# Gated unit of a decoder layer: squared positive part moved from VectorE to ScalarE

## The chip, the cores and the metric

One core of one Trainium2 chip runs the whole program. The metric is the device time of one execution in microseconds, the median of several. A core has five engines with a queue each, which work in order: TensorE (PE, with its weight loads as PEld), VectorE (DVE), ScalarE (ACT), GpSimd (POOL) and SyncE (SP, which issues the DMAs). They are kept in step by semaphores alone.

## The reference

A decoder of two layers on x of shape (16, 128, 128): past attention, block attention and a routed expert layer (layer 0), then a gated attention unit, a one-head attention and a top-1 expert layer (layer 1), each followed by a layer norm. The change is in the gated unit:

```python
    uv = jax.nn.silu(xn @ uv_w.T)
    u = uv[..., :E]; v = uv[..., E:2 * E]; base = uv[..., 2 * E:]      # E = 256, base 128 wide
    base = base[:, :, None, :] * gamma[None, None] + beta
    base = _rope_seq(base)
    q = base[:, :, 0]; k = base[:, :, 1]
    qk = jnp.einsum('bis,bjs->bij', q, k)
    qk = qk + w_rel[idx][None]
    kernel = jnp.square(jax.nn.relu(qk / sqrt_s))                      # 128 x 128 for each of 16 sequences
    out = u * jnp.einsum('bij,bje->bie', kernel, v)
    out = out @ o_w.T
    return x * res_scale + out
```

## The kernel before

The 16 sequences go through the late stages in 8 pairs. `late_pe`, `late_act`, `late_dve` and `late_pool` write out each engine's queue by hand: for t = 1 to LATE_STEPS each calls the `step(t)` of the gated unit (Gau), of the one-head attention (One, pair 0 at t = 8) and of the top-1 experts (Top, pair 0 at t = 16). A `step(t)` runs several stages, each on the pair t - back, and the order in its tuple is the order in the queue. Step 0 of the gated unit is done inside the last group of the routed experts (`moe.group`).

In the gated unit a pair p goes this way. ScalarE scales x (L2308, waits for GpSimd's layer norm) and, behind TensorE's transposes (L2237), copies it out of PSUM (L2316). TensorE projects it to the base (L2246), u (L2250) and v (L2254); ScalarE applies Silu to each (L2324, L2328, L2332). The rope is two products and a sum: VectorE multiplies the base by the cosine table (L2348), GpSimd multiplies its swapped half by the sine table (L2415) and adds the beta table (L2418), and VectorE adds both (L2357). TensorE forms q k (L2262) into PSUM bank 3. `kernel_matrix` on VectorE adds the relative bias (L2370) into `biased` and, after a wait for that, computes max(biased, 0) * biased into `kern` (L2375). TensorE multiplies v by it (L2273, "average"), VectorE gates the result with u (L2384), TensorE applies the output weights (L2286), and VectorE adds the kept x (L2364 keeps it, L2394 adds), with the layer norm's statistics (L1706, L1715). `biased` and `kern` have two buffers, so pair p uses that of pair p - 2.

The orders in a step t, as pair numbers relative to t:

- TensorE: project t-1, transpose x of t, average t-3, output t-4, q k of t-2;
- ScalarE: scale x of t, the three Silus of t-1, copy x of t;
- VectorE: kernel matrix t-3, add output t-5, keep t-1, cosine product t-1, rope sum t-1, gate t-3;
- GpSimd: sine product and beta t-1, and at t = 3, 4, 5 a third each of the layer norm of the last four sequences (L1767 to L1778, `late_ln_norm`), then the One stage's statistics and normalisations.

At t = 8, behind the gated unit's step, ScalarE runs a small Exp (L2879), ahead of which its table is loaded; a small Silu did the same ahead of step 0 (L1972), and a small Gelu does at t = 17 (L2882).

Of the kernel before, what the change touches and what calls it, by code (L numbers as in the profile page):

```python
# [22 lines left out]
ALU = mybir.AluOpType  # L23
ACT = mybir.ActivationFunctionType
# [37 lines left out]
def pipelined(eng, stages, count=B):  # L62


    deepest = max(lag for lag, _ in stages)
    peel = deepest + 2 + deepest % 2

    def step(n, parity):
        for lag, stage in stages:
            i = n - lag  # L70
            if not isinstance(i, int) or 0 <= i < count:
                stage(i, (parity - lag) % 2)

    for n in range(min(peel, count)):
        step(n, n)
    if peel < count:
        with eng.Fori(peel // 2, count // 2) as half:
            step(half * 2, 0)
            step(half * 2 + 1, 1)
    for n in range(count, count + deepest):  # L80
        step(n, n)
# [39 lines left out]
def declare(nc, ctx):  # L121
    c = Chip()
# [205 lines left out]
    s.own("ln2_", "aggr ln")  # L328
    for n in range(3, 7):
        s.own("ln%d_" % n, "stats aggr ln")  # L330
    s.own("gau_", "keep")
    s.own("top_", "xn")
    s.own("moe_", "xn x_turned x_t logits_prod route_d route_p exp gates_turned gates_t gates_out scaled prod out_t out_turned out "
                  + " ".join("row%d" % q for q in range(SPREAD)))
# [393 lines left out]
def attention_act(c, act, ph, more=None, tail=None):  # L728
# [58 lines left out]
    def window(t):  # L787

        if cross:
            if t in (4, 8):  # L790
                high_of("q", 0, t // 4 + 1)
            if t in (5, 9):
                high_of("k", 1, t // 4 + 1)
            if t == 7:
                copy_x(3)
            return
        if t % 4 == 0 and t < 12:
            high_of("q", 0, t // 4 + 1)
        if t % 4 == 1 and t < 12:
            high_of("k", 1, t // 4 + 1)  # L800
        if t == 6:
            high(c, act, "past_", 0, c.b_rk[:, 0:1], c.rq_parts[:, 3])
        if t in (10, 14, 16):
            high_rq({10: 0, 14: 1, 16: 2}[t])
        if t in (7, 11, 15):
            copy_out({7: 0, 11: 1, 15: 2}[t])
# [13 lines left out]
    def slot(t):  # L820
# [4 lines left out]
        if cross and t == 4:  # L825
            copy_x(2)
# [24 lines left out]
        if more:  # L851
            more(t)

    return SlotsACT(begin, slot, high_of, copy_x, copy_neg, rows, copy_norm, copy_out, high_rq)


# [937 lines left out]
def turn_bank(c, g):  # L1794

    return c.banks[:, 2 if g else 6, :]
# [120 lines left out]
class MoeACT:  # L1917
# [4 lines left out]
    def copy_x(self, g):  # L1922
        c, act, s = self.c, self.act, self.s
        act.wait_ge(*s.after("moe_x_turned", g + 1))
        self.nc.scalar.copy(c.out_T[:, g * GROUP:(g + 1) * GROUP], turn_bank(c, g)).then_inc(s["moe_x_t"], 1)
# [290 lines left out]
def lag(t, start, back):  # L2216

    p = t - start - back
    return p if 0 <= p < PAIRS else None


def both(x):

    return x.unsqueeze(1).broadcast_to([P, 2, P])


class GauPE:
# [62 lines left out]
    def step(self, t):  # L2290
        for stage, back in ((self.project, 1), (self.turn_x, 0), (self.average, 3), (self.output, 4), (self.product, 2)):
            if lag(t, 0, back) is not None:
                stage(lag(t, 0, back))


class GauACT:
# [4 lines left out]
    def scale_x(self, p):  # L2301
# [4 lines left out]
        for v in range(2):  # L2306
            i = 2 * p + v
            self.nc.scalar.activation(c.x_s[:, p % 2, v, :], column(c.Y[:, i:i + 1, :]), ACT.Identity, bias=c.shift2[:, i:i + 1],  # L2308
                                      scale=c.scale2[:, i:i + 1]).then_inc(s["gau_xs"], 1)

    def copy_x(self, p):
        c, act, s = self.c, self.act, self.s
        act.wait_ge(*s.after("gau_x_turned", p + 1))
        if p >= 2:
            act.wait_ge(*s.after("gau_v_prod", p - 1))
        self.nc.scalar.copy(c.x_T[:, p % 2, :], c.banks[:, 2, 0:PAIR]).then_inc(s["gau_x_t"], 1)  # L2316
# [15 lines left out]
        self.nc.scalar.activation(c.v2[:, p % 3].rearrange("p v e -> p (v e)"), c.banks[:, 7, :], ACT.Silu).then_inc(s["gau_v"], 1)  # L2332

    def step(self, t):
        for stage, back in ((self.scale_x, 0), (self.silu, 1), (self.copy_x, 0)):
            if lag(t, 0, back) is not None:
                stage(lag(t, 0, back))


class GauDVE:  # L2340
# [26 lines left out]
    def kernel_matrix(self, p):  # L2367
        c, dve, s = self.c, self.dve, self.s
        dve.wait_ge(*s.after("gau_qk", p + 1))
        self.nc.vector.tensor_tensor(c.biased[:, p % 2], c.banks[:, 3, 0:PAIR].rearrange("p (v t) -> p v t", v=2),  # L2370
                                     both(c.rel_bias[:, :]), ALU.add).then_inc(s["gau_biased"], 1)
        dve.wait_ge(*s.after("gau_biased", p + 1))
        if p >= 2:
            dve.wait_ge(*s.after("gau_av", p - 1))
        self.nc.vector.scalar_tensor_tensor(c.kern[:, p % 2], c.biased[:, p % 2], 0.0, c.biased[:, p % 2], ALU.max, ALU.mult)\  # L2375
            .then_inc(s["gau_kernel"], 1)

    def gate(self, p):
        c, dve, s = self.c, self.dve, self.s
# [530 lines left out]
def program(nc, a, gates, out):  # L2910
    with ExitStack() as ctx:
        c = declare(nc, ctx)
        load_first = [(c.w_qk, "w_qk"), (c.b_qk, "b_qk")]
        load_turn = [(c.ident_b, "ident_b"), (c.w_v, "w_v"), (c.b_v, "b_v"), (c.ident_f, "ident_f")]
# [230 lines left out]
```

## Time and profile before

| | |
|---|---|
| median of 3 runs | 563.93 us (561.54 to 566.16) |
| the profiled execution's own time | 562.95 us |
| its span | 560.5 us, 14081 instructions |
| VectorE busy | 453.5 us (81%), 1021 instructions |
| ScalarE busy | 334.1 us (60%), 579 instructions |
| GpSimd busy | 217.6 us (39%), 333 instructions |
| chain of waits | TensorE 66%, VectorE 16%, ScalarE 5%, GpSimd 2% |

The span runs from the first to the last instruction of the profiled execution. Busy shares are means over the whole span; the gated unit takes the stretch from about 450 to 504 us. The chain of waits is followed back from the last instruction: at each step to what released it, or to the instruction before it on its engine. A time in brackets with an arrow is idle time of the engine just before the instruction and what ended it. Merged rows (x2, x8) span from the first start to the last end.

### The profile page before, as it was taken

The page shows a single profiled execution, that of the slowest core. Times are in us where ns is not written, and L with a number is a line of the kernel's source. Part 1 is how long each engine was busy: PE and PEld are TensorE (multiplying, and loading weights), DVE is VectorE, ACT ScalarE, POOL GpSimd, SP SyncE. Part 2 cuts the span into 40 slices and gives each one's busy share as a digit, 9 for nine tenths or more (in the row PEclk, how much of TensorE's full clock was granted, in tenths as well). Part 3 has the DMA queues.
Part 4 walks back from the last instruction along what each step waited for, and adds up shares of the span by engine and source line. Part 5 has one row for each costly group of instructions (what it writes and reads, how often), then busy time and mean ns, then how long its engine had stood idle before and what let it go on. Part 6 is the DMA issues. An engine that isn't in the chain of part 4 may idle for free.

```text
span 560.5 us, 14081 instructions
## 1 busy us (share of the span) xinstructions
PE 511.9 (91%) x5230; PEld 280.6 (50%) x5230; DVE 453.5 (81%) x1021; ACT 334.1 (60%) x579; POOL 217.6 (39%) x333
## 2 busy tenths in 40 slices
PE   2799898999999999999999999889999998999894
PEld 1355563233333333333333666654544467879793
DVE  4678788889889898989884789768678757988897
ACT  3267765577787778777876767561101254446881
POOL 7213312511122421340233445064253376887543
PEclk9799999799999999999999999899999998999999
DMA  4556520230002203030302143017746800001001
GB/s 129 134 134 162 152 61 2 58 100 4 21 20 59 73 5 100 2 101 3 95 11 64 42 117 106 12 49 244 264 141 216 299 19 2 2 19 39 2 20 56
DMA packets 48303, 44.04 MB, mean 79 GB/s; under 512 B 7207, under 2 KB 39207, under 8 KB 48231
## 3 DMA queue, kind: packets, MB, share of 16 engines
q1 hardware_dynamic: 46220, 42.40, 25.7%
q10 hardware_dynamic: 2016, 0.75, 0.5%
q8 instruction: 42, 0.69, 0.5%
q14 instruction: 25, 0.20, 0.1%
HBM read 25.18 MB, written 1.18 MB: 47 GB/s over the span
## 4 chain that ended last, share of the span: by engine, by line
PE 66%; DVE 16%; issue 6%; ACT 5%; DMA 3%; POOL 2%; ACTq 1%; SPq 1%; DVEq 0%; POOLq 0%
PE banks L1240 13%; PE banks L1220 8%; PE banks L1155 5%; PE banks L1865 5%; PE banks L574 5%; PE banks L474 4%; PE banks L531 3%; DVE rec_negmax L1469 2%; DVE negmax L898 2%; PE banks L557 2%; DMA past_mem<-gates 2%; PE banks L1251 2%; DVE shared L1988 2%; ACT probs L742 1%; PE banks L2273 1%
## 5 line engine op out<-in xcount | busy, mean ns | idle before, releaser
L1469 DVE TENSOR_REDUCE rec_negmax<-banks 128x2 bf16<-128x512 f32 x256 | 164.9, 687 | 22.0 <-PE banks L1155 19.9
L1362 ACT ACTIVATE probs<-banks 128x1024 f32<-128x1024 f32 x128 | 131.0, 1024 | 47.6 <-PE banks L1220 46.7
L1155 PE MATMUL banks<-shared 62*128 62x512 bf16 x256 | 96.2, 391 | 4.2 <-DVE rec_negmax L1469 3.3
L1220 PE MATMUL banks<-shared 64*128 64x256 bf16 x512 | 97.2, 277 | 0.0
L898 DVE TENSOR_REDUCE negmax<-banks 128x8 bf16<-128x1024 f32 x64 | 78.1, 1221 | 19.2 <-PE banks L531 18.6
L1240 PE MATMUL banks<-probs,past_mem 128*32 128x256 f32 x1024 | 83.0, 396 | 1.3 <-ACT o_T L1369 1.3
L742 ACT ACTIVATE probs<-banks 128x1024 f32<-128x1024 f32 x64 | 65.1, 1018 | 27.9 <-PE banks L557 27.4
L1220 PEld LDWEIGHTS banks<-shared 64*128 64x128 bf16 x512 | 30.1, 94 | 69.6 <-issue 65.0
L1865 PE MATMUL banks<-shared,w_r 128*128 128x512 f32 x128 | 59.4, 601 | 1.5 <-DVE shared L1988 1.2
L1988 DVE TENSOR_TENSOR shared<-past_mem,out_T 128x512 f32<-128x512 f32 x64 | 43.2, 694 | 12.0 <-DMA past_mem<-gates 10.9
L574 PE MATMUL banks<-probs,shared 128*32 128x128 f32 x1024 | 42.1, 283 | 0.9 <-ACT probs L742 0.9
L531 PE MATMUL banks<-shared 62*128 62x128 bf16 x512 | 26.2, 223 | 12.3 <-DMA shared<-qk_parts 5.8
L1865 PEld LDWEIGHTS banks<-shared,w_r 128*128 128x128 f32 x128 | 22.5, 190 | 28.7 <-DVE shared L1988 15.2
L1240 PEld LDWEIGHTS banks<-probs,past_mem 128*32 128x32 f32 x1024 | 20.5, 108 | 29.7 <-issue 26.5
L1580 POOL TENSOR_TENSOR rctx<-o 128x128 f32<-128x128 f32 x16 | 7.3, 453 | 68.0 <-DVE o L1491 67.7
L1155 PEld LDWEIGHTS banks<-shared 62*128 62x128 bf16 x256 | 23.6, 93 | 19.5 <-DVE rec_negmax L1469 16.7
L1734 POOL TENSOR_SCALAR ln_tmp<-mv 128x4 f32<-128x4 f32 (+1 forms) x27 | 7.9, 292 | 61.7 <-DVE mv L1715 35.6
L557 PE MATMUL banks<-shared 64*128 64x128 bf16 x512 | 25.5, 219 | 4.6 <-ACT probs L742 4.6
L574 PEld LDWEIGHTS banks<-probs,shared 128*32 128x32 f32 x1024 | 24.5, 110 | 9.5 <-ACT probs L742 1.7
L1735 POOL TENSOR_TENSOR rstd<-ln_tmp,minus_half 128x4 f32<-128x4 f32 (+1 forms) x27 | 27.0, 1000 | 2.3
L1784 POOL TENSOR_SCALAR Y<-Y,mv,rstd 128x128 f32<-128x128 f32 x32 | 27.5, 870 | 0.7
L446 POOL CAST qk_parts<-left 128x512 bf16<-128x512 f32 x14 | 8.5, 610 | 47.7 <-DVE left L427 47.7
(261 smaller groups left out, 955.2 us busy)
## 6 DMA issues: line engine op xcount, KB each, us to landing
past_mem<-gates SPq DMA_DIRECT2D x64, 256.0 KB, 4.7
shared<-qk_parts SPq DMA_DIRECT2D x84, 128.0 KB, 2.7
shared<-past_mem SPq DMA_DIRECT2D x30, 128.0 KB, 2.9
shared<-qk_parts SPq DMA_DIRECT2D x18, 64.0 KB, 2.1
shared<-rec_neg_T SPq DMA_DIRECT2D x64, 2.0 KB
Y<-in_x SPq DMA_DIRECT2D x4, 256.0 KB, 3.1
xk_T<-in_ctx_T SPq DMA_DIRECT2D x4, 256.0 KB, 3.4
w_r<-in_w_r SPq DMA_DIRECT2D x4, 256.0 KB, 3.1
```

What stands on the lines that cost most here:

```text
L531: last = nc.tensor.matmul(c.max_banks[r][:, a * P:(a + 1) * P], c.QT[64 * r:64 * r + 62, gp, j, at_:at_ + P], c.KT[64 * r:64 * r + 62, gp, ...
L557: last = nc.tensor.matmul(c.score_banks[r][:, a * P:(a + 1) * P], c.KT[64 * r:64 * r + 64, gp, j, at_:at_ + P], c.QT[64 * r:64 * r + 64, g ...
L574: last = nc.tensor.matmul(c.ctx_bank[HV * q:HV * (q + 1), half * P:(half + 1) * P], c.V_rows[:, i % 4, head_rows(8 * half + 2 * q + a)], c ...
L742: nc.scalar.activation(c.probs[:, (2 * i + half) % 4, :], c.score_pairs[0], ACT.Exp, scale=HEAD_SCALE)\
L898: nc.vector.tensor_reduce(c.negmax[:, i % 2, :].rearrange("p (r j) -> p r j", r=2)[:, :, 4 * half:4 * half + 4], c.max_pair.rearrange("p ( ...
L1155: self.nc.tensor.matmul(c.max_banks[r], c.QT[64 * r:64 * r + 62, g % 2, j, off:off + P], c.rKT[64 * r:64 * r + 62, j, :], start=True, stop ...
L1220: last = self.nc.tensor.matmul(c.score_pairs[i % 2][:, r * 512 + a * PAIR:r * 512 + (a + 1) * PAIR], c.rKT[64 * r:64 * r + 64, 2 * g + a, ...
L1240: last = self.nc.tensor.matmul(c.ctx_bank[HV * q:HV * (q + 1), past * PAIR:(past + 1) * PAIR], c.rV_rows[:, t, head_rows(8 * (g // 2) + 2 ...
L1362: nc.scalar.activation(c.probs[:, i % 4, :], c.score_pairs[i % 2], ACT.Exp, scale=HEAD_SCALE)\
L1469: self.nc.vector.tensor_reduce(out, c.max_banks[r].rearrange("p (a t) -> p a t", a=NP_PAST), AX_X, ALU.max, negate=True).then_inc(s["rec_m ...
L1865: self.nc.tensor.matmul(sum_bank(c, g), c.w_r[:, e, :], c.scaled[:, n % RING, :], start=False, stop=(e == NE - 1)).then_inc(s["moe_prod"], 1)
L1988: self.nc.vector.tensor_tensor(c.scaled[:, n % RING, :], c.gate_rows[:, n % SPREAD, :], c.out_T[:, g * GROUP:(g + 1) * GROUP], ALU.mult).t ...
```

## The change

VectorE keeps the sum with the bias. The product max(biased, 0) * biased is replaced by two ScalarE activations of 128x256, Relu from `biased` to `kern` and Square of `kern` in place. They stand in ScalarE's queue behind the scaling of x and ahead of the Silus. VectorE waits, ahead of the sum, for Relu of two pairs before (a new semaphore `gau_relu`), as ScalarE does for the average of two pairs before.

```diff
-    s.own("gau_", "keep")
+    s.own("gau_", "keep relu")
...
 class GauACT:
+    def kernel_matrix(self, p):
+        c, act, s = self.c, self.act, self.s
+        act.wait_ge(*s.after("gau_biased", p + 1))
+        if p >= 2:
+            act.wait_ge(*s.after("gau_av", p - 1))
+        kern = c.kern[:, p % 2].rearrange("p v t -> p (v t)")
+        self.nc.scalar.activation(kern, c.biased[:, p % 2].rearrange("p v t -> p (v t)"), ACT.Relu).then_inc(s["gau_relu"], 1)
+        act.wait_ge(*s.after("gau_relu", p + 1))
+        self.nc.scalar.activation(kern, kern, ACT.Square).then_inc(s["gau_kernel"], 1)
...
     def step(self, t):
-        for stage, back in ((self.scale_x, 0), (self.silu, 1), (self.copy_x, 0)):
+        for stage, back in ((self.scale_x, 0), (self.kernel_matrix, 3), (self.silu, 1), (self.copy_x, 0)):
...
 class GauDVE:
     def kernel_matrix(self, p):
         dve.wait_ge(*s.after("gau_qk", p + 1))
+        if p >= 2:
+            dve.wait_ge(*s.after("gau_relu", p - 1))
         self.nc.vector.tensor_tensor(c.biased[:, p % 2], c.banks[:, 3, 0:PAIR].rearrange("p (v t) -> p v t", v=2),
                                      both(c.rel_bias[:, :]), ALU.add).then_inc(s["gau_biased"], 1)
-        dve.wait_ge(*s.after("gau_biased", p + 1))
-        if p >= 2:
-            dve.wait_ge(*s.after("gau_av", p - 1))
-        self.nc.vector.scalar_tensor_tensor(c.kern[:, p % 2], c.biased[:, p % 2], 0.0, c.biased[:, p % 2], ALU.max, ALU.mult)\
-            .then_inc(s["gau_kernel"], 1)
```

## Rows read from the trace of the kernel before

**Rows 1.** The page: busy us, share of the span, instructions.
```profile
PE 511.9 (91%) x5230; PEld 280.6 (50%) x5230; DVE 453.5 (81%) x1021; ACT 334.1 (60%) x579; POOL 217.6 (39%) x333
```

**Rows 2.** Windows: busy of PE, PEld, DVE, ACT, POOL; PEclk, DMA share, GB/s.
```profile
485.00:490.00 5.00, 4.38 (x31) 3.91 (x30) 4.86 (x13) 1.72 (x4) 4.76 (x5) 1.00 0.02 5
```

**Rows 3.** Timeline of VectorE: start us, us, engine, line, operation, tiles [idle before].
```profile
462.28 1.64 DVE L2357 TENSOR_TENSOR shared<-shared 128x512 f32<-128x512 f32 x1
463.84 0.41 DVE L2370 TENSOR_TENSOR shared<-banks,rel_bias 128x256 f32<-128x256 f32 x1
...
473.43 0.69 DVE L2357 TENSOR_TENSOR shared<-shared 128x512 f32<-128x512 f32 x1 [2.57 <-POOL shared L2418]
474.04 0.68 DVE L2384 SCALAR_TENSOR_TENSOR shared<-banks,shared 128x512 f32<-128x512 f32 x1
474.64 0.41 DVE L2370 TENSOR_TENSOR shared<-banks,rel_bias 128x256 f32<-128x256 f32 x1
...
486.37 0.41 DVE L2370 TENSOR_TENSOR shared<-banks,rel_bias 128x256 f32<-128x256 f32 x1
486.82 0.42 DVE L2375 SCALAR_TENSOR_TENSOR shared<-shared 128x256 f32<-128x256 f32 x1
487.16 0.60 DVE L2394 SCALAR_TENSOR_TENSOR Y<-Y,rstd,banks 128x128 f32<-128x128 f32 x2
...
492.22 0.41 DVE L2370 TENSOR_TENSOR shared<-banks,rel_bias 128x256 f32<-128x256 f32 x1
...
496.95 0.41 DVE L2370 TENSOR_TENSOR shared<-banks,rel_bias 128x256 f32<-128x256 f32 x1
...
500.40 0.42 DVE L2370 TENSOR_TENSOR shared<-banks,rel_bias 128x256 f32<-128x256 f32 x1 [0.65 <-PE banks L2262]
```

**Rows 4.** Chain of waits in order of time: start us, us, what.
```profile
497.39 0.44 DVE shared L2375
497.87 1.16 PE banks L2273 x8
...
502.19 0.89 PE banks L2273 x8
```

**Rows 5.** By line: duration ns min/median/max, first and last start us, forms.
```profile
L2415 POOL TENSOR_TENSOR shared<-shared,rope_sin x8: 1272/1476/1718, 454.9 to 491.5; 128x512 f32<-128x512 f32 x8
L2418 POOL TENSOR_TENSOR shared<-shared,rope_beta x8: 1262/1268/1597, 456.7 to 492.9; 128x512 f32<-128x512 f32 x8
L2316 ACT COPY shared<-banks x8: 367/368/380, 446.8 to 487.5; 128x256 f32<-128x256 f32 x8
L1972 ACT ACT_TABLE_LOAD  x1: 1283/1283/1283, 436.6 to 436.6; - x1
```

**Rows 6.** Timeline of ScalarE.
```profile
480.27 0.88 ACT L2308 ACTIVATE shared<-Y,shift,scale 128x128 f32<-128x128 f32 x2 [3.10 <-POOL shift L1778]
481.05 0.57 ACT L2324 ACTIVATE shared<-banks 128x512 f32<-128x512 f32 x1
```

**Rows 7.** Timeline of GpSimd.
```profile
461.98 1.40 POOL L2415 TENSOR_TENSOR shared<-shared,rope_sin 128x512 f32<-128x512 f32 x1 [0.75 <-ACT shared L2324]
...
472.06 1.27 POOL L2418 TENSOR_TENSOR shared<-shared,rope_beta 128x512 f32<-128x512 f32 x1
...
477.06 1.27 POOL L2418 TENSOR_TENSOR shared<-shared,rope_beta 128x512 f32<-128x512 f32 x1
...
479.98 0.20 POOL L1778 TENSOR_TENSOR shift<-ln_tmp,scale 128x4 f32<-128x4 f32 x1
481.76 1.27 POOL L2415 TENSOR_TENSOR shared<-shared,rope_sin 128x512 f32<-128x512 f32 x1 [1.58 <-issue]
```

**Rows 8.** Timeline of TensorE.
```profile
465.39 1.91 PE L2273 MATMUL banks<-shared 128*128 128x128 f32 x8 [2.18 <-DVE shared L2375]
```

**Rows 9.** Windows, columns as in rows 2.
```profile
466.00:467.00 1.00, 1.00 (x7) 1.00 (x6) 0.96 (x2) 0.00 (x0) 0.54 (x1) 0.50 0.06 16
...
468.00:469.00 1.00, 1.00 (x4) 0.82 (x4) 0.80 (x4) 0.00 (x0) 0.00 (x0) 0.50 0.00 0
```

## The prediction

> **What bounds the kernel now.** I read the page's busy shares first: TensorE 91%, VectorE 81%, ScalarE 60% [rows 1]. These are averages over stages with different limits, so they don't price a change to one stage. The edited lines work only in the gated unit, from the first sum with the bias at 463.8 us to the eighth at 500.4. The windows there show VectorE busy 4.86 of 5.00 us, TensorE 4.38 and ScalarE 1.72 [rows 2]. The timeline of VectorE gives the step: the fifth sum starts at 486.37, the sixth at 492.22, so 5.85 us, with no idle between its instructions [rows 3]. VectorE is the bound of these steps, and ScalarE has room.
>
> The chain of waits tells what the stage hands on. It goes through VectorE up to the seventh kernel matrix, which starts at 497.39, then into TensorE's products with v at 497.87, and it is still on TensorE with the eighth at 502.19 [rows 4]. From there it is TensorE work of the next stage. So the time at which the seventh average starts is what the change moves, and nothing behind it has slack to give a delay back.
>
> **The change part by part.** Eight instructions leave VectorE (L2375, 0.42 us each). In the step shown the bias sum starts at 486.37, the removed instruction at 486.82 and the next at 487.16 [rows 3]. Without a wait, the next instruction starts about 0.34 behind the sum too, so VectorE saves 0.79 - 0.34 = 0.45 us a step, 5.85 to 5.40.
>
> ScalarE gets 16 activations of 128x256 float32 from SBUF to SBUF. No such row exists. The nearest is its copy of the same shape out of PSUM, 368 ns [rows 5]; twice the columns with Silu take 0.57 [rows 6]. These are my bounds for one, and since the shape is that of the copy I take 0.40, a little for the SBUF source. Square waits for Relu, with a step of 0.04 between as from VectorE's sum to the instruction that reads it [rows 3]. The matrix is then ready 0.41 + 0.04 + 0.40 + 0.04 + 0.40 = 1.29 us after the sum starts, against 0.45 + 0.42 = 0.87 now: 0.42 later for TensorE. With the bounds it is 1.23 to 1.63. The new wait of VectorE on Relu of two pairs ago and ScalarE's wait on the average of two pairs ago are both over by a whole step, so they cost nothing. No DMA is issued or moved.
>
> Do the activations need another table? ScalarE's load takes 1283 ns [rows 5], and one lies ahead of Silu and one ahead of Exp; no row shows whether Relu and Square work with either. I take none. The Trainium skill (ScalarE: Activation LUTs, section on table sets) says that relu, copy and identity are filler in every set and does not list square there; the trace agrees for the copies, which run here between Silus.
>
> **Where it goes wrong is the place.** ScalarE's order in a step is now: scale x of pair t, kernel matrix of pair t-3, Silu of pair t-1, copy x. Behind the new wait stand the three Silus and the copy. The first Silu feeds GpSimd's two multiplies by the rope tables (L2415, L2418), these feed VectorE's rope sum (L2357), and in VectorE's order the gate (L2384) and the next bias sum stand behind that. So there is a closed loop: bias sum, kernel matrix, Silu, GpSimd, rope, gate, next bias sum. Today Silu doesn't wait for the sum, and VectorE's own work sets the step. The loop's length:
>
> - sum to the start of Silu: 0.41 + 0.04 + 0.40 + 0.04 + 0.30 = 1.19 us. Silu doesn't read the square, and activations without a dependence start about 0.10 before the last ends (two scalings of 0.88 in all from 480.27, and Silu at 481.05 [rows 6]);
> - start of Silu to start of GpSimd: 481.05 to 481.76, 0.71 [rows 6, 7];
> - GpSimd: 1.48 + 0.08 + 1.27 = 2.83, the medians of the two multiplies [rows 5] and the step between two of its instructions;
> - GpSimd's end at 472.06 + 1.27 = 473.33 to the rope sum at 473.43: 0.10 [rows 3, 7];
> - rope to gate 0.61, gate to the next sum 0.60 [rows 3].
>
> Together 6.04 us. VectorE's 5.40 fits into this, and so does TensorE (4.38 of 5 us, hence about 5.1 a step). VectorE would idle some 0.6 us a step for L2418.
>
> The sum, from the first bias sum to the seventh. The start gains: the rope sum at 462.28 took 1.64 because GpSimd had begun its next multiply at 461.98 [rows 3, 7]; that multiply now waits for Silu, so the rope takes its 0.69 and the first bias sum starts at 462.89 instead of 463.84, 0.95 earlier. Six loops are 36.2. Once there is a detour: the last four GpSimd layer norm steps of the fourth group run behind L2418 in one step and end with the shift, from 478.33 (477.06 + 1.27) to 480.18, and then the scaling of x, which stands ahead of the kernel matrix [rows 6, 7]. I take 1.5 for them without VectorE beside them, 0.09 to the scaling and 0.78 for it: Relu starts 2.37 after L2418's end, against 0.10 + 0.61 + 0.60 + 0.41 + 0.04 = 1.76 normally, so +0.6. The seventh sum starts at 462.89 + 36.2 + 0.6 = 499.7; today it starts at 496.95 [rows 3], so +2.8. The matrix comes 0.42 later behind it: +3.2 us at the average. At the eighth matrix nothing is added: it needs 1.29 behind its sum, and TensorE reaches it 1.8 us after (500.40 to 502.19 [rows 3, 4]).
>
> The profiled execution took 562.95 us, span 560.5; the median of the runs is 563.93, 1 us above, and they spread from 561.54 to 566.16. The forecast is 562.95 + 3.2 = about **566.2 us**, by the median 567.1.
>
> The bounds. Both activations lie in the loop, so with 0.37 and 0.57 it is 5.98 and 6.38: -0.4 to +2.0 over six. With GpSimd undisturbed, at its shortest times (1.27 + 0.08 + 1.26 [rows 5]), it is 0.22 less, -1.3 over six; with both multiplies at their longest (1.72 and 1.60) 0.57 more, +3.4. The detour is 0 to 1.0.
>
> The Trainium skill (ScalarE: Activation LUTs, rules for kernel authors) says to put relu, max and mul on VectorE and not on ScalarE, which speaks against this change; the trace's prices have the same sign, 0.74 us of ScalarE for 0.42 of VectorE.
>
> **The rivals.**
>
> 1. *VectorE's relief wins* (the other side). VectorE is saturated at 5.85 a step, and ScalarE is idle two thirds of the time [rows 2]. If the loop is shorter than VectorE's remaining 5.40, each of the five saturated steps gives its 0.45: -2.3 us, **560.7**. It decides at a loop of 5.40, which is 0.6 below my sum; each term has a row, and only the activations don't. Against it also: in the step where the rope sum waited, it waited 2.57 us for GpSimd although Silu was not held [rows 3]. Chance 0.15.
>
> 2. *The loop closes, but GpSimd runs undisturbed in it.* L2415 takes from 1.27 to 1.72 [rows 5], and VectorE, now idle ahead of each rope sum, disturbs it less. At its shortest times the loop is 5.82, and the loss 3.2 - 1.3 = 1.9: **564.9**. The Trainium skill (GPSIMD Engine Reference, specifications) says that GpSimd's SBUF interfaces are shared with VectorE's instructions with two SBUF inputs, and the removed instruction is one; the trace agrees in that the rope sum of two SBUF inputs took 1.64 beside L2415. Chance 0.15.
>
> 3. *TensorE's clock falls as well.* It stood idle for 2.18 us ahead of the first average, at 465.39 [rows 8], and its granted clock then was 0.50, the 1.2 GHz level, up to 469 [rows 9]: 3.6 us, in which half the work is lost, 1.8. The new order has a gap of about 0.9 us in each step and of some 1.5 ahead of the seventh average, where TensorE is the bound right after. 3.2 + 1.8 = 5.0: **568.0**. Against it: today's steps, with TensorE idle for 0.6 of 5 us, kept the clock at 1.00 [rows 2]. Chance 0.15.
>
> 4. *Table loads.* If one of the two functions isn't in Silu's table, each of six steps needs two loads inside the loop, 2.57 us: +15 on top, **582**. Chance 0.03.
>
> The forecast, with its own range of 563.5 to 569, keeps 0.52.
>
> **How the numbers follow.** About 1% (5.6 us) is what a measurement of this kernel tells from no change. Faster by that isn't in reach of any case: the eight removals are 3.6 us in all; 0.05 for what I overlook and for the scatter of the runs. Slower by over 1% needs 569.6: the table loads (0.03), half of the clock case (0.07), and in the forecast's case slow activations or a disturbed GpSimd (0.09), together 0.19. The rest, 0.76, is within 1%. The range from 561.8 to 570 leaves out most of rival 1, the table loads and a little of the others.
>
> **What would show it.** Right: Silu (L2324) starts about 1.2 us after each bias sum; Relu's idle ahead is released by VectorE; VectorE's rope sum waits for L2418 in nearly every step; the bias sums stand 6.0 us apart; the seventh average is about 3 us later, and from it on the two traces run parallel. The removed instruction's time shows as idle on VectorE and not as a shorter step. Wrong: bias sums 5.4 us apart with VectorE still full (rival 1); L2415 and L2418 at 1.27 each (rival 2); a granted clock of 0.5 near 502 us (rival 3); ACT_TABLE_LOAD more than at its present places (rival 4). Activations of 0.6 us or more from SBUF would put the time above 569.

## The result, and the profile after

| | before | after |
|---|---|---|
| median of the runs shared by the two | 563.4 us (561.54 to 566.16, 4 runs) | 570.2 us (568.23 to 573.36, 4 runs) |
| profiled execution | 562.95 us, span 560.5 | 568.23 us, span 566.3 |
| first to seventh bias sum | 33.11 us | 39.05 us |
| seventh average starts | 497.87 | 503.48 |
| from the first Silu of the gated unit to the end of the span | 106.3 us | 111.9 us |

The ratio after to before is 1.0134, interval 1.0095 to 1.0173: slower by 1.3%. The forecast was 566.2, with a range up to 570.0 and a chance of 0.19 for slower by over 1%. It had the mechanism and had it too small: 3.2 us forecast at the seventh average, 5.6 measured. Ratios here and below go by the fast executions alone (one of the kernel with the matrix behind the Silus took 974 us and is left out of its ratio), and they are not quotients of the medians printed beside them.

The last row of the table is what I use for single profiles below and call the **stretch**. The first Silu starts anywhere from 452.6 to 460.7 us in the profiled executions of this study, for reasons that lie ahead of the edited stage, so a whole span is a poor measure of an edit, and its end less that start a better one. It is still one execution each: three of the same kernel after gave 111.4, 111.9 and 113.2, and that of before holds a stretch at the lower clock [rows 9] that after's first doesn't.

The page's busy times of after, as in [rows 1]: VectorE has lost 8 instructions and 8.3 us, ScalarE has gained 16 and 4.9 us.

```profile
PE 511.2 (90%) x5230; PEld 278.9 (49%) x5230; DVE 445.2 (79%) x1013; ACT 339.0 (60%) x595; POOL 218.7 (39%) x333
```

One of the windows inside the stage, columns as in [rows 2] (length, busy of PE, PEld, DVE, ACT, POOL, granted clock, DMA share, GB/s). VectorE was busy for 4.86 of 5.00 us there and is now busy for 2.44; nobody else is full. When the bound engine loses half its work time and the steps get longer, the steps are set by a chain that goes round through several engines.

```profile
485.00:490.00 5.00, 4.54 (x30) 3.94 (x28) 2.44 (x6) 2.02 (x6) 4.33 (x4) 1.00 0.00 0
```

The chain itself, once round, in the timelines of after (start, duration, engine, line, operation, tiles, idle before). ScalarE: Relu waits for VectorE's sum, and the Silu of base (L2334) starts 476.92 - 475.70 = 1.22 us after that sum.

```profile
476.15 0.42 ACT L2317 ACTIVATE shared<-shared 128x256 f32<-128x256 f32 x1 [2.95 <-DVE shared L2382]
476.60 0.42 ACT L2319 ACTIVATE shared<-shared 128x256 f32<-128x256 f32 x1
476.92 0.58 ACT L2334 ACTIVATE shared<-banks 128x512 f32<-128x512 f32 x1
```

GpSimd: its multiply by rope_sin (L2422) starts 0.71 after that Silu, and here takes 2.03 us.

```profile
471.33 1.73 POOL L2422 TENSOR_TENSOR shared<-shared,rope_sin 128x512 f32<-128x512 f32 x1 [1.55 <-issue]
473.13 1.27 POOL L2425 TENSOR_TENSOR shared<-shared,rope_beta 128x512 f32<-128x512 f32 x1
...
477.63 2.03 POOL L2422 TENSOR_TENSOR shared<-shared,rope_sin 128x512 f32<-128x512 f32 x1 [0.94 <-POOL scale L1773]
479.74 1.26 POOL L2425 TENSOR_TENSOR shared<-shared,rope_beta 128x512 f32<-128x512 f32 x1
```

VectorE: the rope sum (L2367) idles 2.56 us for GpSimd, and behind it stand the gate (L2391) and the next bias sum (L2382). Read the cosine product (L2358) as well: in five of the six rounds between the first and the seventh sum it starts within 0.22 us of L2422. The idle time of the rope sum is far more than the 0.6 us a step that I had forecast; why is told further below.

```profile
471.23 0.69 DVE L2358 TENSOR_TENSOR shared<-shared,rope_cos 128x512 f32<-128x512 f32 x1 [0.89 <-ACT shared L2334]
474.49 0.69 DVE L2367 TENSOR_TENSOR shared<-shared 128x512 f32<-128x512 f32 x1 [2.57 <-POOL shared L2425]
475.10 0.69 DVE L2391 SCALAR_TENSOR_TENSOR shared<-banks,shared 128x512 f32<-128x512 f32 x1
475.70 0.42 DVE L2382 TENSOR_TENSOR shared<-banks,rel_bias 128x256 f32<-128x256 f32 x1
...
477.35 0.58 DVE L2374 SCALAR_TENSOR_TENSOR Y<-Y,mv,res_scale 128x128 f32<-128x128 f32 x2
477.85 0.68 DVE L2358 TENSOR_TENSOR shared<-shared,rope_cos 128x512 f32<-128x512 f32 x1
481.09 0.69 DVE L2367 TENSOR_TENSOR shared<-shared 128x512 f32<-128x512 f32 x1 [2.56 <-issue]
...
482.30 0.41 DVE L2382 TENSOR_TENSOR shared<-banks,rel_bias 128x256 f32<-128x256 f32 x1
...
502.12 0.41 DVE L2382 TENSOR_TENSOR shared<-banks,rel_bias 128x256 f32<-128x256 f32 x1
```

The bias sums start at 463.07, 469.41, 475.70, 482.30, 489.20, 495.81, 502.12 and 506.02. TensorE, which answers to [rows 4]: it idles 1.94 us ahead of the seventh average, waiting for Square.

```profile
503.48 1.16 PE L2273 MATMUL banks<-shared 128*128 128x128 f32 x8 [1.94 <-ACT shared L2319]
```

### The profile page after: what moved, and what is told of

Same layout as the page of the kernel before. It is cut to its first block and busy times, and to the rows that moved or that the text cites. A ratio compares the mean times of both kernels' runs of the same rounds, so it can differ in the third digit from the quotient of the medians.

```text
span 566.3 us, 14095 instructions
## 1 busy us (share of the span) xinstructions
PE 511.2 (90%) x5230; PEld 278.9 (49%) x5230; DVE 445.2 (79%) x1013; ACT 339.0 (60%) x595; POOL 218.7 (39%) x333
```

## The experiments

All kernels but two were timed in five rounds against the kernel before; after itself had three, and its third look is one run. "Sums" is the time from the first bias sum to the seventh in the profiled execution. In the profiles of before, of before with keep first and of the matrix behind the Silus, TensorE's granted clock fell to 0.50 for some 3 us behind the first average; in the others it didn't. What that is worth in their stretches is worked out below.

| kernel | ratio to before (interval) | stretch, us | sums, us |
|---|---|---|---|
| before | 1 | 106.3 | 33.1 |
| after | 1.0134 (1.0095 to 1.0173) | 111.9 | 39.1 |
| after, once more | 1.0105 (1.0061 to 1.0150) | 113.2 | 38.8 |
| after, third look | one run | 111.4 | 38.5 |
| matrix behind the Silus | 1.0143 (1.0097 to 1.0189) | 112.4 | 38.4 |
| before with the wait alone | 1.0075 (1.0048 to 1.0101) | 109.3 | 37.1 |
| before with the work alone | 1.0007 (0.9973 to 1.0040) | 105.7 | 32.3 |
| after, keep first | 1.0121 (1.0074 to 1.0169) | 110.9 | 38.0 |
| after, short cosine product | 1.0050 (1.0022 to 1.0077) | 107.9 | 35.9 |
| after, Silu of base first | 1.0007 (0.9982 to 1.0033) | 104.8 | 31.0 |
| after, Silu of base first, keep first | 1.0051 (1.0023 to 1.0079) | 105.6 | 31.7 |
| after, Silu of base first, gate early | 1.0011 (0.9983 to 1.0039) | 105.3 | 31.5 |
| before, keep first | 1.0012 (0.9980 to 1.0043) | 107.6 | 34.4 |

### Is it the place of the matrix in ScalarE's order?

```diff
-        for stage, back in ((self.scale_x, 0), (self.kernel_matrix, 3), (self.silu, 1), (self.copy_x, 0)):
+        for stage, back in ((self.scale_x, 0), (self.silu, 1), (self.copy_x, 0), (self.kernel_matrix, 3)):
```

> The kernel after, with the kernel matrix moved to the end of ScalarE's step, behind the three Silus and the copy; nothing else changes. Theory (the loop: the Silu stands behind the wait for the bias sum, so GpSimd's multiplies start late): the loop opens, Silu no longer waits for the sum of its own step, bias sums are 5.3 to 5.6 us apart, and the time is at or below that of the kernel before: ratio 0.995 to 1.002. Rival 1 (the two activations cost what they cost by their own time on the way to TensorE, wherever they stand): ratio 1.008 to 1.014 as in the kernel after. Rival 2 (the loss lies outside the gated unit): also 1.01.

Measured: 571.25 us, ratio 1.0143, no better than the change, so this expectation failed. The Silus no longer wait for the sum and GpSimd's multiplies are at 1.27, yet from the third on the bias sums stand 6.80 us apart. ScalarE in this kernel, one step (columns as above):

```profile
483.17 0.60 ACT L2342 ACTIVATE shared<-banks 128x512 f32<-128x512 f32 x1 [0.26 <-PE banks L2254]
483.66 0.37 ACT L2326 COPY shared<-banks 128x256 f32<-128x256 f32 x1
483.92 0.43 ACT L2317 ACTIVATE shared<-shared 128x256 f32<-128x256 f32 x1
...
488.25 0.60 ACT L2334 ACTIVATE shared<-banks 128x512 f32<-128x512 f32 x1 [2.69 <-PE banks L2246]
```

And its TensorE:

```profile
482.11 1.03 PE L2254 MATMUL banks<-w_v,shared 128*128 128x256 f32 x4
482.97 0.38 PE L2237 MATMUL banks<-ident_f,shared 128*128 128x128 f32 x2
484.85 1.16 PE L2273 MATMUL banks<-shared 128*128 128x128 f32 x8 [1.49 <-ACT shared L2319]
...
487.18 1.03 PE L2246 MATMUL banks<-shared,w_ub 128*128 128x256 f32 x4
```

Another chain has closed. The matrix stands behind the Silu of v, which waits for TensorE's product L2254; TensorE's average L2273 waits for the matrix; and the next pair's products, L2246 first, stand behind the average. One round is 6.80 us. So the place of the wait matters on both sides: behind TensorE's late products it is as bad as ahead of the Silus. The theory of the loop through Silu was neither shown nor refuted by this kernel, which needed a cleaner cut.

### How much is the wait, how much the work?

One kernel has only the wait: the kernel before, whose ScalarE waits for VectorE's finished matrix of pair t-3 where the change has its two activations.

```diff
+    def held(self, p):
+        self.act.wait_ge(*self.s.after("gau_kernel", p + 1))
...
-        for stage, back in ((self.scale_x, 0), (self.silu, 1), (self.copy_x, 0)):
+        for stage, back in ((self.scale_x, 0), (self.held, 3), (self.silu, 1), (self.copy_x, 0)):
```

> The kernel before (VectorE computes both parts of the kernel matrix), and in ScalarE's queue, where the two activations stand in the kernel after, only a wait for the kernel matrix of pair t-3. ScalarE does no work for it. Theory: the loop is closed as well, shorter by the difference of 1.22 and about 0.90 us from the bias sum to the start of Silu: about 6.0 us with GpSimd at 3.1, so some 0.3 x 6 = 2 us below the kernel after and 3 to 4 us above before: ratio 1.005 to 1.008. Rival 1 (the activations' own time): no loss, ratio 0.999 to 1.002.

Measured: 566.71 us, ratio 1.0075, stretch +3.0; the ratio is as expected. The other kernel has only the work: two activations of the same size at the same place, on a tile that needs no sum.

```diff
+    def spare(self, p):
+        act.wait_ge(*s.after("gau_square", p))
...
+        self.nc.scalar.activation(rctx, ctx, ACT.Relu).then_inc(s["gau_relu"], 1)
+        act.wait_ge(*s.after("gau_relu", p + 1))
+        self.nc.scalar.activation(rctx, rctx, ACT.Square).then_inc(s["gau_square"], 1)
...
-        for stage, back in ((self.scale_x, 0), (self.silu, 1), (self.copy_x, 0)):
+        for stage, back in ((self.scale_x, 0), (self.spare, 3), (self.silu, 1), (self.copy_x, 0)):
```

> The kernel before, with two more activations of 128x256 in ScalarE's queue where the change has them, but on a tile that is already there (Relu of ctx, Square in place), so that they wait for no sum; VectorE keeps its own square. It has ScalarE's added work without the added wait. Theory (the wait behind the sum costs, the 0.83 us of work does not): ScalarE idles over 2 us in each step, so stage from first Silu to end 106 to 107.5 us against 106.3, ratio 0.999 to 1.002. Rival (the two activations' own time costs: 8 x 0.83 us, of which what is not hidden lengthens each step): ratio 1.003 to 1.013, stage 108 to 112.

Measured: 561.24 us, ratio 1.0007, stretch 105.7. ScalarE does all the added work (its two lines, L2315 and L2317 there, have 3.3 us busy each) and it costs nothing measurable; the interval leaves room for up to 0.4%. The wait without any work costs over half of the loss.

The stretches need a correction before they are compared, because the clock fell behind the first average in before's profile and in neither of these two. First average of the kernel with the work alone:

```profile
471.02 1.16 PE L2273 MATMUL banks<-shared 128*128 128x128 f32 x8 [2.25 <-DVE shared L2383]
```

From there to the third bias sum the clock makes the difference: the first two rounds took 10.80 us in before and 10.79 in before with keep first, where it fell, and 9.30 here, where it was kept. So before's stretch would be about 104.8 without the fall, by my estimate from these rounds, and the losses are about 4.5 for the wait, 0.9 for the work and 7.1 for both. That is 1.7 more than the two alone; the two profiles of after in which the clock was kept differ by 0.5. A reason that fits, not shown by itself, is that work which is hidden beside other work isn't hidden inside a closed loop: behind the wait, Silu starts 0.90 us after the sum with the wait alone and 1.22 with both, 1.9 us over six rounds. The ratios (1.0075, 1.0007 and 1.0105 to 1.0134) point the same way, but their intervals are too wide to show it.

In the kernel with the wait alone GpSimd's two multiplies took only 1.27 us each in the step below, and still the steps were 6.0 to 6.3 us. The expectation had 3.1 us of GpSimd for that, which holds for the first two rounds alone. Its VectorE shows why; L2367 there is the keep, a pair of 128x128 instructions with two SBUF inputs:

```profile
482.34 0.41 DVE L2373 TENSOR_TENSOR shared<-banks,rel_bias 128x256 f32<-128x256 f32 x1
...
484.44 2.29 DVE L2367 SCALAR_TENSOR_TENSOR Y<-Y,mv,res_scale 128x128 f32<-128x128 f32 x2
486.66 0.68 DVE L2351 TENSOR_TENSOR shared<-shared,rope_cos 128x512 f32<-128x512 f32 x1
```

Its GpSimd in the same step:

```profile
483.97 1.27 POOL L2418 TENSOR_TENSOR shared<-shared,rope_sin 128x512 f32<-128x512 f32 x1 [1.78 <-issue]
485.32 1.27 POOL L2421 TENSOR_TENSOR shared<-shared,rope_beta 128x512 f32<-128x512 f32 x1
```

Here VectorE comes to the keep 2.10 us after the sum, 0.45 later than in after, and GpSimd to its multiply 1.63 after it, 0.30 earlier. GpSimd had begun first, and the keep took 2.29 us instead of 0.58. In after it is the other way round. One of the two engines pays.

### What does VectorE beside GpSimd cost in the loop?

The cosine product over 2 of 128 columns; the rest of its work is missing. The order and the waits are those of after.

```diff
-        self.nc.vector.tensor_tensor(c.turned[:, p % 2], ...
-                                     c.rope_cos[:, :, :].unsqueeze(2).broadcast_to([P, 2, 2, P]), ALU.mult)
+        self.nc.vector.tensor_tensor(c.turned[:, p % 2, :, :, 0:2], ...
+                                     c.rope_cos[:, :, 0:2].unsqueeze(2).broadcast_to([P, 2, 2, 2]), ALU.mult)
```

> The kernel after, with VectorE's cosine product over 2 of 128 columns (the rest of the rope is left out, so this part of the work is missing). It measures what lies beside GpSimd's multiply. Theory that the cosine product, with two SBUF inputs, lengthens the multiply from 1.27 to 1.73 us: 1.27 in the first three steps, where nothing else of VectorE lies beside it, and the loop is 0.45 shorter: 2 to 3 us below the kernel after, ratio 1.006 to 1.009. Rival (length has another source): the multiply keeps 1.7 and the time stays within 0.5 us of the kernel after, since the cosine product itself isn't in the loop.

Measured: 565.25 us, ratio 1.0050, stretch 107.9, 4.0 less than after: the direction of the theory, and somewhat more than its 2 to 3 us. Its GpSimd:

```profile
481.94 1.27 POOL L2422 TENSOR_TENSOR shared<-shared,rope_sin 128x512 f32<-128x512 f32 x1 [2.35 <-issue]
483.29 1.27 POOL L2425 TENSOR_TENSOR shared<-shared,rope_beta 128x512 f32<-128x512 f32 x1
487.82 1.43 POOL L2422 TENSOR_TENSOR shared<-shared,rope_sin 128x512 f32<-128x512 f32 x1 [1.55 <-issue]
```

Where both multiplies are at 1.27, and outside the detour, the bias sums are 5.81 to 5.83 us apart, the length that the prediction's second rival gave the loop. VectorE idled over 2 us a step in after, so the 0.5 us of work that the cut saves there can't be the gain by itself; it comes through GpSimd. Next, the order of VectorE, to take the keep out of L2422's way:

```diff
-        for stage, back in ((self.kernel_matrix, 3), (self.add_out, 5), (self.keep, 1), (self.turn, 1), (self.rope, 1), (self.gate, 3)):
+        for stage, back in ((self.kernel_matrix, 3), (self.keep, 1), (self.add_out, 5), (self.turn, 1), (self.rope, 1), (self.gate, 3)):
```

> The kernel after, with VectorE's keep moved ahead of add_out, so that it runs before GpSimd's first multiply begins. In the kernel after that multiply took 1.73 us beside the cosine product alone, and 2.03 in the two steps in which keep lay beside it too. Theory that the neighbours on VectorE lengthen GpSimd's multiply: 1.73 in all steps, 0.6 to 0.9 us less than the kernel after, ratio about 1.011 against 1.0125. Rival (the multiply's length has another source): 2.03 stays in two steps and the time too.

Measured: 569.23 us, ratio 1.0121; stretch 1.0 less than after, within the scatter of after's own three (111.4 to 113.2). The expected 1.73 in all steps came in three of the six rounds (1.77, 1.72, 1.72). No multiply takes 2.03 any more, but in the other three it is at 1.27 or 1.28 and now the cosine product pays, with 1.53 to 1.58. VectorE and then GpSimd in one step:

```profile
484.14 1.58 DVE L2358 TENSOR_TENSOR shared<-shared,rope_cos 128x512 f32<-128x512 f32 x1
```

```profile
483.90 1.27 POOL L2422 TENSOR_TENSOR shared<-shared,rope_sin 128x512 f32<-128x512 f32 x1 [0.94 <-POOL scale L1773]
485.25 1.59 POOL L2425 TENSOR_TENSOR shared<-shared,rope_beta 128x512 f32<-128x512 f32 x1
...
490.64 1.72 POOL L2422 TENSOR_TENSOR shared<-shared,rope_sin 128x512 f32<-128x512 f32 x1 [2.34 <-issue]
```

### Is one Silu all of it?

The three Silus are split: that of base goes ahead of the matrix, those of u and v stay behind it. The two activations, the wait and VectorE's shorter list are all still there.

```diff
-    def silu(self, p):
+    def silu_base(self, p):
...
+    def silu(self, p):
...
-        for stage, back in ((self.scale_x, 0), (self.kernel_matrix, 3), (self.silu, 1), (self.copy_x, 0)):
+        for stage, back in ((self.scale_x, 0), (self.silu_base, 1), (self.kernel_matrix, 3), (self.silu, 1), (self.copy_x, 0)):
```

> The kernel after, with only the Silu of the base moved ahead of the kernel matrix in ScalarE's step; the Silus of u and v and the copy stay behind it. With the matrix at the very end, the bias sums were 6.8 us apart from the fourth on and TensorE waited 1.49 us a step for Square, since the matrix stood behind the Silu of v, which waits for TensorE's products. Theory (the place in the queue costs, not the work): GpSimd starts without the bias sum, the matrix waits for one product of TensorE only, bias sums 5.3 to 5.6 us apart, first Silu to end of span 105 to 106.5 us (before 106.3, after 111.9), ratio 0.995 to 1.003. Rival (16 activations cost by their own time and place of computation): span part 109 us or more, ratio above 1.007.

Measured: 562.68 us against 562.72, ratio 1.0007 (0.9982 to 1.0033); stretch 104.8. The whole loss is gone. ScalarE of this kernel:

```profile
480.03 0.88 ACT L2308 ACTIVATE shared<-Y,shift,scale 128x128 f32<-128x128 f32 x2 [3.09 <-POOL shift L1778]
480.81 0.57 ACT L2334 ACTIVATE shared<-banks 128x512 f32<-128x512 f32 x1
481.29 0.40 ACT L2317 ACTIVATE shared<-shared 128x256 f32<-128x256 f32 x1
481.73 0.42 ACT L2319 ACTIVATE shared<-shared 128x256 f32<-128x256 f32 x1
```

Silu of base no longer stands behind the sum, so GpSimd, rope and gate don't either. This is the cleanest cut of the study: one instruction moved, 7.1 us of stretch back. The stretch is also 1.5 us below that of before, but this isn't the relief of VectorE that the first rival counted on. It is what the fall of the clock cost in before's profile; here TensorE stood idle for 2.00 us ahead of the first average and kept its clock:

```profile
466.78 1.16 PE L2273 MATMUL banks<-shared 128*128 128x128 f32 x8 [2.00 <-ACT shared L2319]
```

The first two rounds took 8.97 us here, 9.30 with the work alone and 10.80 in before; the next four took 22.03 here and 22.31 in before. So of the 2.1 us between 33.1 and 31.0 at most some 0.6 are left for the relief, and the interval of the timed executions allows for a gain of 1.0 us and a loss of 1.9.

### Is there more in the open loop?

With the loop open, VectorE's keep again took up to 2.56 us beside GpSimd. Two orders of VectorE were tried against that, and the first also on the kernel before. Keep ahead of add_out (the edit shown above), with Silu of base first:

> As the kernel with the base's Silu first, and VectorE's keep ahead of add_out. In the kernel before and in those with free steps, the pair of keeps took 1.6 to 2.7 us where GpSimd's multiply began beside it, instead of 0.6. If keep escapes the multiply, VectorE's step falls towards 5.1 us, where TensorE's own 5.1 sets it: 1 to 2 us below the kernel with the base's Silu first, ratio 0.992 to 0.999. Rival: the instruction that now stands in keep's place (the cosine product, the rope sum) is held as long instead, and nothing is gained.

Measured: 565.21 us, ratio 1.0051, slower than before. The stretch of its one profile, 105.6, doesn't show this loss, so where it lies stays open. The collisions have moved: the cosine product is held for 1.38 in one step, and the keep, in later ones, for 1.62 and 2.79 us. The same order in the kernel before:

> The kernel before, with VectorE's keep ahead of add_out and nothing else. It tells whether what the kernel before loses beside GpSimd is keep's place: if so 1 to 2 us below before, ratio 0.996 to 0.999; if another instruction is held in its stead, 0.999 to 1.002.

Measured: 564.42 us, ratio 1.0012, no difference that can be measured; one keep was held for 2.71. Then the gate ahead of the keep:

```diff
-        for stage, back in ((self.kernel_matrix, 3), (self.add_out, 5), (self.keep, 1), (self.turn, 1), (self.rope, 1), (self.gate, 3)):
+        for stage, back in ((self.kernel_matrix, 3), (self.add_out, 5), (self.gate, 3), (self.keep, 1), (self.turn, 1), (self.rope, 1)):
```

> The changed kernel with the Silu of base ahead of the matrix (as in e5_base_first), and in addition VectorE's gate of step t-3 moved ahead of the keep of step t-1. Theory (with the loop open, the sums stand 5.1 to 5.7 us apart because VectorE and GpSimd hold each other up in turn; what is moved within VectorE's order moves the hold-up elsewhere): stage from the first Silu to the end of the span 104 to 105.5 us, ratio 0.998 to 1.002, no gain over e5_base_first's 104.8. Rival (the two-input keep was what waited, and the gate, which needs only what is long done, fills its place): a stage of 103 us or less, ratio 0.994 or less, GpSimd's multiplies at 1.27 us and the keep at 0.6 us.

Measured: 561.47 us against 561.75, ratio 1.0011, stretch 105.3. The signs of the rival came, and its time did not. From the third round on the multiplies are at 1.27 or 1.28 and the keep is at 0.61 (0.74 once), and VectorE idles instead for TensorE's average, ahead of the gate:

```profile
475.25 0.69 DVE L2394 SCALAR_TENSOR_TENSOR shared<-banks,shared 128x512 f32<-128x512 f32 x1 [0.85 <-PE banks L2273]
475.86 0.61 DVE L2377 SCALAR_TENSOR_TENSOR Y<-Y,mv,res_scale 128x128 f32<-128x128 f32 x2
476.38 0.69 DVE L2361 TENSOR_TENSOR shared<-shared,rope_cos 128x512 f32<-128x512 f32 x1
477.10 0.69 DVE L2370 TENSOR_TENSOR shared<-shared 128x512 f32<-128x512 f32 x1
477.71 0.42 DVE L2385 TENSOR_TENSOR shared<-banks,rel_bias 128x256 f32<-128x256 f32 x1
```

And TensorE is full there, as far as its modelled ends tell. Columns as above:

```profile
472.00:477.00 5.00, 5.00 (x35) 4.67 (x34) 4.05 (x13) 2.67 (x6) 3.71 (x6) 1.00 0.00 2
```

Its queue goes round once in 5.04 us (the product of base starts at 471.34 and 476.38), and the bias sums stand 5.02 to 5.08 apart in four of the six rounds, with 6.05 in the step with the layer norm detour. So with VectorE's collisions gone the step is TensorE's own, about the 5.1 us that the prediction worked out for it. Six such rounds are 30.2 us by this estimate, and the kernel with the Silu of base first took 31.0 with the detour in it; no order of VectorE or ScalarE has much left to win by it. No kernel of the study is shown to be faster than the one before.

### Does TensorE's clock fall?

The change once more, as it is:

> The kernel after, unchanged, on the same chip and beside the same runs of the kernel before as the others. Its profile gave 111.9 us from the first Silu to the end of the span, against 106.3, so 5.6 us or 1.0%; the first comparison said 1.34%. If the whole loss lies in that part, the ratio is near 1.010; if something ahead of it is slower too, near 1.013 again, and the first Silu starts more than 1 us later than in the kernel before.

Measured: 568.50 us, ratio 1.0105, what the stretch alone had led me to expect. The first Silu came at 457.79 us, 3.6 later than in before, so the scatter ahead of the stage is larger than what this sign was to tell. In this profile the seventh average starts after a gap of 1.95 us and takes 2.07 us, and the granted clock is 0.50, the 1.2 GHz level, for some 3 us behind it:

```profile
506.65 2.07 PE L2273 MATMUL banks<-shared 128*128 128x128 f32 x8 [1.95 <-ACT shared L2319]
```

Windows of one us, columns as above:

```profile
507.00:508.00 1.00, 1.00 (x6) 1.00 (x6) 0.01 (x1) 0.34 (x2) 0.90 (x2) 0.50 0.00 0
...
509.00:510.00 1.00, 1.00 (x7) 1.00 (x7) 0.45 (x1) 0.00 (x0) 1.00 (x3) 0.58 0.00 0
```

The eighth sum comes 5.40 us after the seventh and not 3.90, so a fall costs 1.5 us. A third look at the same kernel:

> The changed kernel as it is, for a further look at TensorE's clock at the seventh average. If the clock falls only in some executions: the gap ahead of that average is again 1.9 to 2.0 us, and the sum of the seventh step to that of the eighth is either 3.9 us (clock kept) or 5.4 us (clock fallen). If the fall is the rule and the first profile the exception: 5.4 us again.

```profile
505.17 1.16 PE L2273 MATMUL banks<-shared 128*128 128x128 f32 x8 [1.95 <-ACT shared L2319]
```

The same gap, the clock kept, 3.89 us to the eighth sum. So behind the seventh average it fell in one of three profiled executions.

## Why the prediction was wrong

**What held.** The place in ScalarE's queue decided. The closed loop that was named is the one in the trace, Silu following the sum by 1.22 us (1.19 forecast) and the rope waiting for GpSimd in nearly every step. The start held: the first bias sum was forecast at 462.89, and it came at 463.07, with the stage itself 0.19 later in this execution. The detour held: its step is 6.90 us against 6.29 and 6.34 of steps with multiplies of the same length, so 0.6. The matrix's own delay held: sum to average is 503.48 - 502.12 = 1.36 against 0.92, so 0.44 (0.42 forecast). Relu and Square took 0.42 each for the 0.40 assumed, and no table was loaded for either. From the seventh average on the traces run parallel: 62.6 us to the end before, 62.8 after.

**The step that failed** is the loop's third term, "GpSimd: 1.48 + 0.08 + 1.27 = 2.83, the medians of the two multiplies". In the six loops the multiplies by rope_sin took 1.77, 1.73, 2.03, 1.73, 2.03 and 1.27, those by rope_beta 1.27, 1.27, 1.26, 1.27, 1.26 and 1.79. With six steps of 0.08 that is 19.16 us for the 16.98 forecast: 2.2 us more. The six loops together are 39.05 for 36.84, also 2.2 more; every other term is within 0.2. Adding the 0.19 of the late start gives 5.6 for 3.2. The experiment with the short cosine product shows the term from the other side: with almost nothing left to collide the loop is 5.82.

Why the median misled: the eight rows behind [rows 5] mix two situations, and the closed loop makes one of them in all but its last step. Silu releases the cosine product on VectorE and the multiply on GpSimd at once, VectorE begins 0.10 us before GpSimd, and GpSimd pays. Inside the stage the trace of before had one step in just this state, the one in which the rope idled for 2.57 us [rows 3] (and ahead of the first sum that of pair 0, at 454.90, with 1.72 as well), and its multiply could have been read there. GpSimd of before:

```profile
470.27 1.72 POOL L2415 TENSOR_TENSOR shared<-shared,rope_sin 128x512 f32<-128x512 f32 x1 [3.73 <-issue]
```

With 1.72 for 1.48 the loop is 6.28 and the forecast 1.4 us later, 567.6. The further 0.3 of the 2.03 comes where the keep is still running as the multiply starts, and was not to be had from any step of before. It isn't certain either: in the third look the same meeting went the other way in the third and the fifth round, the multiply took 1.44 and 1.43 and the cosine product 1.77 and 1.76, and the six rounds were 38.5 instead of 39.1.

**A reading that was wrong without moving the sum.** I took VectorE's 5.85 us a step for its own work, and expected it to idle for 0.6 in the new loop; ahead of the rope sum alone it idled for 2.56 in five of the six rounds. Part of the 5.85 was VectorE held beside GpSimd. The keep took 1.66 to 2.10 us in three of before's steps, and 0.60 or 0.61 where no multiply ran beside it; the step with 0.61 in it was 4.73 long. The keep of before:

```profile
482.43 2.10 DVE L2364 SCALAR_TENSOR_TENSOR Y<-Y,mv,res_scale 128x128 f32<-128x128 f32 x2
```

So a busy share of 4.86 in 5.00 was no measure of VectorE's load. The forecast didn't turn on it, since VectorE wasn't what bounded the new loop, but the 5.40 at which the first rival was to be decided did.

**The rivals.** *VectorE's relief wins*: no; the first seven sums are 6.3 to 6.9 apart. *GpSimd undisturbed*: the reverse. I argued that an idle VectorE disturbs GpSimd less; but it is idle after its cosine product, not during it. *The clock falls as well*: in one of three profiles behind the seventh average, for 1.5 us (forecast 1.8). *Table loads*: no.

**The median.** In the medians after is 6.8 us above before, in the first profiles 5.3. Two things that the profiles show would do that: a fall of the clock in some executions of after, worth 1.5 us, and before's own profile, which had such a fall behind the first average while other executions of before may have had none. Plain scatter would do it too: the interval reaches down to 5.4 us, and the second comparison of the same kernel gave 568.5 against 562.7, 5.8 apart. The timed executions have on record only the mean clock of the whole span (0.977 to 0.988 for after, in no order with the times), so how often the clock falls in this stage stays open. That 570.2 lies just above the range and 568.5 inside it is chance; the 2.2 us that the loop's third term was short of is not.

## What to carry to other kernels

When work moves to an idle engine, ask which of that engine's queued instructions now stand behind its wait, and follow them until they come back to what is waited for; here the work by itself cost nothing that could be measured, the wait by itself over half of the loss, and the rest seems to come from where the work stood inside the round that the wait had closed. If the round closes, take each term from a row that is in the state the loop will make, one step of it if there is only one, and not from a median over all states. And compare the granted clock of the two profiles stage by stage before you read a gain of one or two us from them. The repair is in the order: split off the one instruction that other engines need early, and put it ahead of the wait.

## What the runs showed of the hardware that I had not expected

**VectorE and GpSimd take turns, they don't slow each other down.** With the multiply by rope_sin at 471.33 and the cosine product from 471.23 to 471.92 in after, the multiply ends at 473.06, 1.14 us after the cosine product. In the step with 2.03 it ends at 479.66, and the cosine product at 478.53: 1.13. In the kernel with keep first it is 492.36 and 491.23: 1.13. So the multiply does nearly all of its 1.27 us after VectorE has finished. The other way round, with the multiply first (483.90 to 485.17 in that kernel), the cosine product runs to 485.72, 0.55 behind the multiply's end, and the next multiply, started at 485.25, ends at 486.84, again 1.12 later. The Trainium skill (SBUF — State Buffer, section on who interferes with whom) describes this as an exclusive lock that whoever issues first holds for its whole instruction. The numbers here agree with that, down to the wait alone's keep, which ended 0.14 us after the second multiply.

Reordering VectorE alone brought nothing here: of the two other orders, in four kernels, keep first moved the collisions to other instructions, and gate early took most of them away and left a step that TensorE fills.

**A clock that falls or not after the same gap.** Ahead of the seventh average TensorE idled 1.94, 1.95 and 1.95 us in the three profiles of after, and the granted clock fell to 0.50 in the second only. The first average shows the same: behind gaps of 2.18 (before), 2.18 (before, keep first) and 2.00 us (matrix behind the Silus) the clock fell, and behind 2.25 (work alone), 2.00, 2.00 and 1.99 us (the three kernels with the Silu of base first) it didn't. A gap of that size is a risk to be priced by its chance, not a yes or no.
